# Shared expert and gate as three float32r products of split rows and split weights

## The reference

```python
x = _layernorm(x + attention(x, kernel, WO))          # attention ends in einsum('bsf,fm->bsm', out, WO[0])
flat = x.reshape(-1, 256)
probs = softmax(flat @ gate_W)                        # gate_W: 256 x 8
topk_w, topk_idx = top_k(probs, 2)                    # then divided by their sum
out = 0.5 * gelu(flat @ shared_W + shared_b)          # shared_W: 256 x 256
for e in range(8):
    h = gelu(flat @ W1[e] + b1[e])
    out = out + combine[:, e:e + 1] * (h @ W2[e] + b2[e])
x = _layernorm(x + layernorm(out) * gamma + beta)
```

## Time and profile before

| | before |
|---|---|
| three executions | 1952.67, 1954.52, 1955.86 us, median 1954.52 |
| the profiled execution | 1952.68 us |
| its span, from first to last instruction | 1950.9 us |
| granted TensorE clock, mean | 0.979 of full |
| TensorE, VectorE, ScalarE busy | 1849.5, 1354.6, 992.6 us |
| token stage | about 1268 to 1421 us |

### The profile page before, as it was taken

One profiled execution on the slowest core, in us unless ns is written; L12 is line 12 of the kernel. 1 busy time (PEld: TensorE's weight loads), 2 busy tenths in 40 slices (PEclk: granted clock), 3 DMA queues, 4 the chain that ended last, 5 costly groups with the idle time before them and its releaser, 6 DMA issues. The chain is left out here.

```text
span 1950.9 us, 31310 instructions
## 1 busy us (share of the span) xinstructions
PE 1849.5 (95%) x11143; PEld 1180.5 (61%) x11143; DVE 1354.6 (69%) x1737; ACT 992.6 (51%) x1432; POOL 338.4 (17%) x354
## 2 busy tenths in 40 slices
PE   7999999999999999999999999989837999999986
PEld 5445444444444444444444444488827999999982
DVE  5676767677767677767676777866675666666656
ACT  5555454555454555544555445445514555555547
POOL 1000000000000000000000000000005777777764
PEclk9999999999999999999999999999968999999998
DMA  5000000000000000120000000054241334333335
GB/s 167 17 28 17 22 17 28 16 23 17 28 17 22 17 28 17 51 71 28 17 22 17 28 20 15 17 190 176 102 158 34 88 88 86 88 86 86 88 52 173
DMA packets 70077, 110.28 MB, mean 57 GB/s; under 512 B 7627, under 2 KB 45709, under 8 KB 67661
## 3 DMA queue, kind: packets, MB, share of 16 engines
q1 hardware_dynamic: 52861, 85.68, 13.0%
q0 software_dynamic: 17104, 23.12, 6.4%
HBM read 70.20 MB, written 38.57 MB: 56 GB/s over the span
## 5 line engine op out<-in xcount | busy, mean ns | idle before, releaser
L415 ACT ACTIVATE a_e<-banks 128x1024 f32<-128x1024 f32 x512 | 496.5, 1022 | 218.2 <-PE banks L307 218.2
L515 DVE TENSOR_TENSOR a_esum<-a_esum,a_e 128x1024 f32<-128x1024 f32 x384 | 469.5, 1223 | 57.4 <-ACT a_e L415 36.3
L321 PE MATMUL banks<-a_e,a_v 128*64 128x512 f32 x2048 | 495.7, 605 | 0.0
L321 PEld LDWEIGHTS banks<-a_e,a_v 128*64 128x64 f32 x2048 | 124.4, 136 | 238.4 <-issue 175.9
L307 PE MATMUL banks<-a_qh,a_kh 64*128 64x512 f32 x1024 | 230.1, 446 | 5.2 <-issue 5.2
L519 DVE RECIPROCAL a_inv<-banks 128x512 f32<-128x512 f32 x64 | 214.9, 3358 | 15.4 <-PE banks L330 15.4
L512 DVE TENSOR_TENSOR a_esum<-a_e 128x1024 f32<-128x1024 f32 x64 | 78.4, 1226 | 202.5 <-ACT a_e L415 202.5
L61 POOL MEMSET t_ident<- 128x128 f32 x1 | 0.2, 204 | 1245.3 <-POOLq L107 1245.3
L307 PE MATMUL banks<-a_qh,a_kl 64*128 64x512 f32 x1024 | 202.3, 392 | 0.0
L307 PE MATMUL banks<-a_ql,a_kh 64*128 64x512 f32 x1024 | 201.8, 391 | 0.0
L1622 ACT ACTIVATE e_g<-banks,e_b1c 128x256 f32<-128x256 f32 x280 | 116.0, 469 | 143.6 <-PE banks L1569 142.9
(11 more groups left out here) (233 smaller groups left out, 3196.3 us busy)
## 6 DMA issues: line engine op xcount, KB each, us to landing
attn_out<-a_ot SPq DMA_DIRECT2D x64, 256.0 KB, 2.0
a_w<-w_qkv SPq DMA_DIRECT2D x32, 256.0 KB, 3.1
raw<-attn_out SPq DMA_DIRECT2D x4, 2048.0 KB, 8.9
t_ot<-attn_out SPq DMA_DIRECT2D x4, 2048.0 KB, 8.7
raw<-w_up SPq DMA_DIRECT2D x8, 1024.0 KB, 5.0
raw<-w_down SPq DMA_DIRECT2D x8, 1024.0 KB, 7.4
raw<-x_t SPq DMA_DIRECT2D x8, 512.0 KB, 9.3
acc_rows<-shared SPq DMA_DIRECT2D x4, 1024.0 KB, 8.9
```

The source lines that it names most:

```text
L321: mm = pe.matmul(o_acc[slot % 2][h * DH:(h + 1) * DH, :], v[quad % 2][:, n, head], e[n % NE][:, h * BANK:(h + 1) * BANK], start=n == 0, st ...
L415: act.activation(e[n % NE], ring[n % 2], ACT.Exp, scale=SCALE).then_inc(e_ok, 1)
L515: dve.tensor_tensor(acc[:, :], acc[:, :], e[n % NE], ALU.add).then_inc(add_ok, 1)
```

## The change

The turned tile and the weights are each split in a float32r value and its float32r remainder, as the projection before does it already. `branch` becomes three products for each of the two blocks: high by high, low by high, high by low. ScalarE's copy writes the high part of the tile (`x2t_h`) and raises a new semaphore; VectorE's new `turned_low` subtracts it from what stands in PSUM, writes `x2t_l`, and raises `x2t_ok`, for which `branch` waits. In VectorE's order `turned_low(n+1)` stands ahead of `biased(n)`. The weights are split once, behind the first four steps of ScalarE and VectorE. In the general path of attention, which is not taken for these inputs, seven semaphores are shared with the other path, so that the number of semaphores suffices.

```diff
-        x2t = [sb(f"t_x2t{u}", [P, KD, P]) for u in range(2)]
+        x2t_h, x2t_l = ([sb(f"t_x2t{what}{u}", [P, KD, P], R32) for u in range(2)] for what in "hl")
+        wgs_h, wgs_l = sb("t_wgs_h", [P, KD, GS], R32), sb("t_wgs_l", [P, KD, GS], R32)
+        x2t_hi, wgs_hi, wgs_ok = sem("t_x2t_hi"), sem("t_wgs_hi"), sem("t_wgs_ok")
...
+                if n == 0:
+                    pe.wait_ge(wgs_ok, 1)
                 for kk in range(KD):
-                    mm = pe.matmul(banks[4 + n % 2][:, 0:GS], x2t[n % 2][:, kk, :], wgs[:, kk, :], start=kk == 0,
-                                   stop=kk == KD - 1)
+                    for m, (lhs, rhs) in enumerate(((x2t_h, wgs_h), (x2t_l, wgs_h), (x2t_h, wgs_l))):
+                        mm = pe.matmul(banks[4 + n % 2][:, 0:GS], lhs[n % 2][:, kk, :], rhs[:, kk, :],
+                                       start=kk == 0 and m == 0, stop=kk == KD - 1 and m == 2)
...
-                act.copy(x2t[n % 2][:, :, :].rearrange("p a b -> p (a b)"), banks[2 + n % 2][:, 0:D]).then_inc(x2t_ok, 1)
+                act.copy(x2t_h[n % 2][:, :, :].rearrange("p a b -> p (a b)"), banks[2 + n % 2][:, 0:D]).then_inc(x2t_hi, 1)
...
+            act.copy(wgs_h[:, :, :], wgs).then_inc(wgs_hi, 1)
...
+            def turned_low(n):
+                dve.wait_ge(x2t_hi, n + 1)
+                dve.tensor_tensor(x2t_l[n % 2][:, :, :].rearrange("p a b -> p (a b)"), banks[2 + n % 2][:, 0:D],
+                                  x2t_h[n % 2][:, :, :].rearrange("p a b -> p (a b)").bitcast(F32), ALU.subtract)\
+                   .then_inc(x2t_ok, 1)
...
+            dve.wait_ge(wgs_hi, 1)
+            dve.tensor_tensor(wgs_l[:, :, :], wgs, wgs_h[:, :, :].bitcast(F32), ALU.subtract).then_inc(wgs_ok, 1)
...
+                if 0 in turned_after(t):
+                    turned_low(0)
                 for n in branched_after(t):
+                    turned_low(n + 1)
                     biased(n)
```

More of the change, by code:

```diff
@@ L555, in attention @@
         g_v_ready = sem("a_g_v_ready")
-        g_s_done = sem("a_g_s_done")
-        g_top_ok = sem("a_g_top_ok")
+        g_s_done = s_done
+        g_top_ok = sum_done
         g_shift_ok = sem("a_g_shift_ok")
-        g_e_done = sem("a_g_e_done")
-        g_inv_ok = sem("a_g_inv_ok")
-        g_e_norm = sem("a_g_e_norm")
+        g_e_done = e_ok
+        g_inv_ok = inv_ok
+        g_e_norm = add_ok
         g_et_done = sem("a_g_et_done")
         g_et_evac = sem("a_g_et_evac")
-        g_pv_done = sem("a_g_pv_done")
-        g_o_evac = sem("a_g_o_evac")
+        g_pv_done = pv_done
+        g_o_evac = o_ok
         g_ot_out = sem("a_g_ot_out")
```

## The result

| | before | after |
|---|---|---|
| median (lowest to highest) | 1954.66 us (1952.67 to 1956.53), 6 runs | 1960.88 us (1958.91 to 1964.10), 6 runs |
| ratio after / before, 95% | | 1.0036, from 1.0025 to 1.0047 |
| the profiled execution, its span | 1952.68, 1950.9 us | 1959.59, 1957.8 us |
| granted TensorE clock, mean | 0.979 | 0.974 |
| TensorE, VectorE, ScalarE busy | 1849.5, 1354.6, 992.6 us | 1847.7, 1365.8, 994.7 us |

The change costs 6.2 us by the medians and 4.9 to 9.2 us by the interval of the ratio (the forecast was +6.7). The steady part of the stage, as in the earlier trace rows: length, busy us (records) of PE, PEld, DVE, ACT and POOL, then the granted clock. TensorE has gone from 106.36 to 99.66 us, and the kernel is slower.

The account below looks back on a forecast made before the run. It took a loop of VectorE and ScalarE waiting for each other, not TensorE, as the bound. 5.7 us in the steady part plus 1.0 at the stage's end gave +6.7, so 1961.2 us, range 1956.5 to 1967.5.

Parts of the forecast that it names:

- The loop: Token stage: VectorE and ScalarE wait in turn; `turned_low` adds 0.35 us, making slots 4.12, at a group's end 6.20.
- the sum: Whole kernel: 23 slots at 0.35 make 8.05, less 2.35 from loads is 5.7; plus 1.0 at the end, +6.7 us.
- the first mark: Biased rows of tile 0; the `turned_low` of slot 6 ahead of it was counted at 0.35 us.
- What the loads give back: Slots waiting for a half's load: shorter waits return 0.25 + 1.05 + 1.05 = 2.35 us of the 8.05.
- waits of 0, 0.1 and 0.5: Load waits holding `ot_high`, expected after the change in place of 0.15, 1.05 and 1.47 us.
- Rival (b): Every half's load swallows 1.05 us, so no change: +3.8, 1958.3 us; chance 0.16 with other ways of being hidden.
- TensorE's saving at nothing: `branch`'s products take 0.16 to 0.18 us less a tile; costed at nothing in slots 6 to 29, as spare time.
- The wait of `branch`: TensorE waits for `turned_low`, up to 2.4 us at a group's end; costed at nothing, two us of slack remaining.
- The end of the stage: Slots 29 to 31 and slot 32's rounds: +1.0 us, from 0.7 to 1.7.
- a sign of being wrong: `turned_low` waiting for ScalarE's copy would mean TensorE lost more of its lead than allowed.
- The rounds of 1.51: Slot 32: biased 0.44, Gelu 0.32, copy 0.40, `turned_low` 0.35 us, four times to tile 30's biased rows.
- Rival (c): TensorE's clock falls at group ends: one slow slot a group gives 1965 us, two 1981; chance 0.10.

Follow-up runs that it names:

- e2: Kernel before plus one more 128x256 addition, read by nobody, ahead of the biased rows on VectorE; 1961.03 us, ratio 1.0038.
- e5: Changed kernel with the subtraction of `turned_low` done twice for 30 of the 32 tiles; 1968.23 us, ratio 1.0074 to before.
- e6: Changed kernel with `turned_low` moved behind the biased rows into VectorE's waits, except in slot 32; 1954.88 us, ratio 1.0009 to before.
- e8: Changed kernel with products nobody reads filling TensorE's gaps ahead of `branch`'s wait; 1960.88 us, ratio 1.0037 to before.
- e7: e6 with ScalarE also copying the next turned tile ahead of Gelu in slot 32; 1953.05 us, ratio 1.0000 to before.
- e4: Changed kernel without `turned_low` (high part taken twice), `branch` waiting for VectorE's statistics where it would begin; 1954.17 us, ratio 1.0003 to before.
- e3: Changed kernel without `turned_low` or its wait, the high part of the rows taken twice; 1950.64 us, ratio 0.9988 to before.
- e12: e9 with attention's and residual's rows on separate semaphores, attention's rows asked for two slots earlier; 1936.61 us, ratio 0.9918 to before.
- e9: e7 with every Gelu on ScalarE one place later; 1947.55 us, ratio 0.9974 to before.
- e10: Kernel before with only every Gelu on ScalarE one place later; 1942.15 us, ratio 0.9953 to before.
- e1: Changed kernel with `turned_low(n+1)` behind `biased(n)` instead of ahead of it; 1960.49 us, ratio 1.0036 to before.

## Why the prediction was right

**The loop.** Right. It named 4.12 and 6.20 us for the slots; they are 4.10 and 6.19, since the subtraction takes 0.33 a slot and not 0.35. e2 shows the price in before's own loop, e5 a second time, and e6 shows that it goes when the same instruction leaves the loop. 23 x 0.33 = 7.6 against the 8.05 of the sum. (The sum counts slots 6 to 28; slot 6's `turned_low` is the 0.3 ahead of the first mark.)

**What the loads give back.** That they give back once is shown (e5), and after, e2 and e8 have at most 0.3 us of waits left. The size was right within 0.35: 2.7 us against 2.35, the waits for loads going from 2.98 in all to 0.29. How it was shared among the loads was not: the prediction left waits of 0, 0.1 and 0.5; the slots with a load (10, 14, 18 and 26) now take 4.21, 4.20, 4.18 and 4.10 us, 0.1 or nothing over an ordinary one. The last, of 0.5, was the wait of slot 26, and it is gone: slot 26 gave back 1.57, more than the 1.05 that three `turned_low` can. The loads of the residual's rows landed 9.5 to 11.8 us behind their issue in these slots of before, and kernels with slots of 3.77 us had waits of 1.3 (e7) to 4.0 (e4) in all. So the close size is partly luck. Rival (b), all given back, fails: the other halves were not waited for, and 23 slots cost 4.95.

**TensorE's saving at nothing.** Right in the slots (e3), by the loop's slack. The Trainium skill, page "Perfetto Trace Analysis", section "Identifying the Most-Contended Engine", points to the engine of highest occupancy, and for TensorE to the share of peak arithmetic and of weight loads in place of matmul time; by this trace the shares of matmuls and of weight loads both point at TensorE (106.36 and 97.25 of 114 us against VectorE's 71.61), and taking work from it gave nothing in the slots, since two engines at 63% and 53% held the pace. In e12, where TensorE is busy 20.00 of 20 us, the rule points at the engine that sets the pace.

**The wait of `branch`.** Right. TensorE waits 17.6 us in all for `turned_low`, up to 2.7 us at a time (predicted: up to 2.4), and by e4 this costs no slot anything.

**The end of the stage.** Put at +1.0, counted from slot 29; the mark of tile 23 stands behind slot 29's `turned_low`, so that +0.65 of it belongs behind the mark, and +0.77 was measured. In its parts: to tile 26's biased rows it is +1.0 (predicted 1.05), and from there, in slot 32, 0.2 less than before (predicted 0.4 less). `turned_low` waits there four times for ScalarE's copy, 0.67 us each; such a wait was named as a sign of being wrong, but in slot 32 it is part of the round that the prediction priced. The rounds of 1.51 were named, and VectorE's timeline of after has three of 1.50 and one of 1.87, where TensorE was at the lower level (0.66 in the stretch):

```profile
1418.72 0.41 DVE L964 TENSOR_TENSOR t_pre<-banks,raw 128x256 f32<-128x256 f32 x1
...
1420.22 0.41 DVE L964 TENSOR_TENSOR t_pre<-banks,raw 128x256 f32<-128x256 f32 x1
...
1421.72 0.41 DVE L964 TENSOR_TENSOR t_pre<-banks,raw 128x256 f32<-128x256 f32 x1
...
1423.59 0.42 DVE L964 TENSOR_TENSOR t_pre<-banks,raw 128x256 f32<-128x256 f32 x1 [0.28 <-PE banks L856]
...
1425.10 0.41 DVE L964 TENSOR_TENSOR t_pre<-banks,raw 128x256 f32<-128x256 f32 x1
...
1426.28 0.42 DVE L964 TENSOR_TENSOR t_pre<-banks,raw 128x256 f32<-128x256 f32 x1 [0.69 <-PE banks L856]
```

```profile
1420.00:1425.00 5.00, 4.61 (x23) 4.15 (x22) 2.70 (x10) 2.03 (x6) 0.00 (x0) 0.66 0.15 52
```

**The clock.** Rival (c) was a true event with no price in the slots. Where it had one the prediction didn't look: behind the stage, as said next. The prediction said that the profile would be wrong if the clock stood below 1.00 between slots 6 and 29; it did, and the slots kept their length. The sentence that "a shorter fall than a slot is hidden altogether" is what held, and e8 shows it from the other side.

**What it had no term for.** 0.85 us behind the stage. They begin with the wait of 1.12 us behind the routing's last products, which ran at the lower level, and the experts give 0.35 back. Nine of the fourteen profiled executions have that wait, of 1.0 to 1.4 us; before, e3, e7, e9 and e10 have none, though e9 and e7 hold the change's work too, and e4 and e6 have it, though their stage ends within 1.5 us of before's. So it doesn't follow from a longer stage; what decides it these runs don't show.

**The sum.** Ahead of the first mark 0.35 was put and 0.3 measured, in the 23 slots 5.7 and 4.95 (about 0.45 less since the subtraction takes 0.33 and not 0.35, and 0.3 less by the loads), behind the mark of tile 23 0.65 and 0.77, behind the stage nothing and 0.85. The misses nearly cancel, and the two profiles lie 6.9 us apart where the sum had 6.7: it came out closer than its worst term, and that is luck. The mechanism isn't, since the slots show it.

## What to carry to other kernels

Look for two engines that wait for each other in turn and add up the steps round the loop. An instruction costs its issue distance (here 0.33 us a tile) if it stands in the loop that binds and nothing if it stands where its engine waits for it anyway, so try another place before dropping it. Relieving the busiest engine gave nothing in the slots here while a tighter loop stood (e3). Two had to be cut before that engine set the pace, Gelu's wait and then the loads, and each cut shows the next loop, in which the same instruction may stand again.

## What the runs showed of the hardware that was not expected

- TensorE's waits at the seven group ends of after were 2.68, 2.10, 2.10, 1.52, 2.09, 1.43 and 2.10 us. In the slots it fell to its lower level (of 1.2 and 2.4 GHz) only behind the third and the fifth; what decides between equal gaps these runs don't show.
- An instruction of VectorE at a group's end cost nothing in e1, since ScalarE's load of the square root's table (1.28 us) runs on beside it.
- Loads of one size, asked for at the same point of the slots, left waits that sum to 1.87 us in one kernel and to 4.04 in another (e3, e4) with the same slots. In this kernel, in which a load ends last now and then, 2 us are luck.
- The last 16 products of the routing took 1.91 us at the full clock in before and 3.22 us in after, mostly at the lower level. VectorE waited for them in nine of the fourteen profiled executions and in five not at all.
